# Narrow attentions: head operands written to DRAM by head, read back 48 partitions at a time; bias first; output products of batch 0 ahead of the last evacuation

## The reference, cut to what matters

```
h   = norm(x)
q   = (h @ Wq + bq) * scale           # 2 x 256 rows, 16 heads of 16
k,v = src @ Wk + bk, src @ Wv + bv    # 2 x 512 (L2, L3) or 2 x 768 (L0) rows
p   = softmax(q @ k.T + mask)         # per batch and head
x   = x + gate * ((p @ v) @ Wo + bo)
```

## Time and profile before

| | us |
|---|---|
| runs, median of 3 | 1135.85 (1135.51 to 1137.48) |
| profiled execution, its own time | 1132.89 |
| span of that execution in the trace | 1131.1 |
| L0a: first instruction, first score, last output product | 14.8, 52.1, 176.3 |
| L2a: first instruction, first score, last output product | 848.3, 878.3, 965.4 |
| L3a: first instruction, first score, last output product | 967.4, 1003.9, 1091.4 |

### The profile page before, as it was taken

One profiled execution on the slowest core, in us unless ns is written; L12 is line 12 of the kernel. 1 busy time (PEld: TensorE's weight loads), 2 busy tenths in 40 slices (PEclk: granted clock), 3 DMA queues, 4 the chain that ended last, 5 costly groups with the idle time before them and its releaser, 6 DMA issues. The chain is left out here.

```text
span 1131.1 us, 17854 instructions
## 1 busy us (share of the span) xinstructions
PE 956.8 (85%) x6548; PEld 809.0 (72%) x6548; DVE 817.2 (72%) x1624; ACT 603.5 (53%) x1367; POOL 336.1 (30%) x325
## 2 busy tenths in 40 slices
PE   4888886569999999997899999998586898478958
PEld 3666665558888889887778989987475566465647
DVE  3377767976787878787578787877664787757865
ACT  2488873034555555553355555655424786257842
POOL 4255541441112222221111222200005454534520
PEclk8889997888999999998899999999788799688989
DMA  5984106140001111111000111000305930296120
GB/s 180 252 130 63 12 1 247 56 162 1 15 24 38 38 39 38 38 38 39 1 4 36 38 38 38 2 1 1 117 1 123 169 44 1 59 191 73 13 80 19
DMA packets 37810, 69.49 MB, mean 61 GB/s; under 512 B 7414, under 2 KB 23288, under 8 KB 35036
## 3 DMA queue, kind: packets, MB, share of 16 engines
q1 hardware_dynamic: 37724, 68.35, 24.7%
HBM read 57.31 MB, written 11.02 MB: 60 GB/s over the span
## 5 line engine op out<-in xcount | busy, mean ns | idle before, releaser
L1230 ACT CAST L1a_probsT_hi<-L1a_bank 128x512 fp32r<-128x512 f32 x128 | 68.8, 589 | 94.3 <-PE L1a_bank L1111 94.3
L1069 POOL TENSOR_SCALAR L1a_wo_hi<-L1a_stage 128x512 fp32r<-128x512 f32 x16 | 10.3, 646 | 363.2 <-PE L1a_sums L74 355.6
L1347 DVE TENSOR_REDUCE L1a_top<-L1a_scores 128x2 f32<-128x1024 f32 x64 | 78.2, 1222 | 36.1 <-PE L1a_scores L74 36.1
L1262 ACT ACTIVATE L1a_probs<-L1a_scores,L1a_neg_max 128x512 f32<-128x512 f32 x128 | 86.8, 684 | 30.6 <-DVE L1a_bias_shifted L1351 25.6
L1285 DVE TENSOR_TENSOR L1a_probsT_lo<-L1a_bank,L1a_probsT_hi 128x512 fp32r<-128x512 f32 x128 | 82.0, 682 | 0.1
L72 PE MATMUL L1a_bank<-L1a_probsT_hi,L1a_v_hi 128*128 128x256 f32 x256 | 73.2, 286 | 9.2 <-DVE L1a_probsT_lo L1285 9.2
L1232 ACT ACTIVATE L1a_attended_hi<-L1a_bank,L1a_cols 128x256 fp32r<-128x256 f32 x64 | 30.5, 476 | 90.4 <-PE L1a_bank L74 90.4
L72 PE MATMUL L1a_bank<-L1a_w_hi,ctxT_hi 128*128 128x256 f32 x256 | 76.5, 299 | 1.1 <-DVE latT_lo L1303 1.0
L74 PE MATMUL L1a_bank<-L1a_w_hi,ctxT_lo 128*128 128x256 f32 x256 | 73.7, 288 | 0.0
L73 PE MATMUL L1a_bank<-L1a_w_lo,ctxT_hi 128*128 128x256 f32 x256 | 73.6, 288 | 0.0
L390 POOL TENSOR_SCALAR L0a_probs<-L0a_probs,L0a_inverse 128x768 f32<-128x768 f32 x64 | 57.2, 906 | 52.9 <-DVE L0a_inverse L641 52.9
(11 more groups left out here) (409 smaller groups left out, 3160.8 us busy)
## 6 DMA issues: line engine op xcount, KB each, us to landing
L1a_stage<-in_L_w SPq DMA_DIRECT2D x15, 1024.0 KB, 4.8
L0m_fold_wq<-in_L_wq SPq DMA_DIRECT2D x2, 2048.0 KB, 19.8
L0a_k_stack<-L0a_k_dram SPq DMA_DIRECT2D x12, 192.0 KB
L0a_w_qkv<-L0a_k_dram SPq DMA_DIRECT2D x12, 192.0 KB
L0a_probs<-in_L_wo SPq DMA_DIRECT2D x1, 2048.0 KB, 9.7
L0a_probsT<-in_L_wo SPq DMA_DIRECT2D x1, 2048.0 KB, 11.2
L0m_stage<-in_L_wm SPq DMA_DIRECT2D x4, 512.0 KB, 5.8
L0m_fold_bias_k<-in_L_bias_k SPq DMA_DIRECT2D x2, 1024.0 KB, 15.4
```

The lines of the kernel that those rows point to most:

```text
L1230: nc.scalar.copy(out, source).then_inc(ring.hi_done, 1)
L1262: nc.scalar.activation(probs[:, g % 2, qt, :], scores[:, qt, :], ACT.Exp, bias=neg_max[:, g % 2, qt:qt + 1], accum_out=row_sum[:, g % 2, q ...
L1347: link(nc.vector.tensor_reduce(top[:, :], scores[:, :, :], AX.X, ALU.max))
```

## The change

1. The DRAM copies have a new layout: `q_dram` and `k_dram` are [octet, head, 48, n], each head with its three groups of 16 rows in the order of the stack. So the high keys and the high queries are written twice: 6 writes an octet in place of 4, each from 128 partitions into 8 blocks of 16 rows; keys first, then the mask, then the queries (each with its own wait).
2. An octet comes back in 4 transfers of 48 partitions x 4 heads and 2 mask rows: 6 in place of 14. The mask rows are issued first, ahead of the wait for the writes. `q_stack` is [128, 2, 4, 256], even and odd heads apart.
3. Loading and splitting: bias and mask are loaded and made right behind the first weight piece; the output weight is split after the keys and queries are evacuated; gate and output bias are loaded and waited for later.
4. POOL clears only the 16 of 32 columns of `v` that stay zero.
5. The output tiles of batch 0 wait only for the products of batch 0, tile 2 only at its last quarter for the last one; DVE adds the output bias to x ahead of the last evacuation.

```diff
-        q_dram = nc.dram_tensor(f"{name}_q_dram", [2, D, ROWS], F32).ap()
-        k_dram = nc.dram_tensor(f"{name}_k_dram", [2, D, B * nk], F32).ap()
+        q_dram = nc.dram_tensor(f"{name}_q_dram", [OCTETS, 8, 3 * DN, Q], F32).ap()
+        k_dram = nc.dram_tensor(f"{name}_k_dram", [OCTETS, 8, 3 * DN, nk], F32).ap()
+        Q_PARTS, K_PARTS = (0, 1, 0), (0, 0, 1)
...
             def write(o):
                 b, kt = divmod(o, KT)
-                ring.wait_evacuated(sp, max(front.index(("q", kt)), front.index(key_jobs[kt, b][-1])))
-                rows = slice(kt * P, (kt + 1) * P)
-                for part in range(2):
-                    for of, at, n, to in ((qT[part][:, kt, :], b * Q, Q, q_dram), (kT[part][:, kt, :], b * nk, nk, k_dram)):
-                        sp.dma_start(to[part, rows, at:at + n], raw(of[:, at:at + n])).then_inc(written[o], 16)
+                ring.wait_evacuated(sp, front.index(key_jobs[kt, b][-1]))
+                for c, part in enumerate(K_PARTS):
+                    heads = k_dram[o, :, DN * c:DN * c + DN, :]
+                    sp.dma_start(heads, raw(kT[part][:, kt, b * nk:(b + 1) * nk])).then_inc(written[o], 16)
                 if o == 0:
                     sp.wait_ge(mask_ready, 1)
-                    sp.dma_start(mask_dram, raw(mask_row[:, :, :])).then_inc(written[o], 16)
+                    sp.dma_start(mask_dram, raw(mask_row[:, :, :])).then_inc(mask_written, 16)
+                ring.wait_evacuated(sp, front.index(("q", kt)))
+                for c, part in enumerate(Q_PARTS):
+                    heads = q_dram[o, :, DN * c:DN * c + DN, :]
+                    sp.dma_start(heads, raw(qT[part][:, kt, b * Q:(b + 1) * Q])).then_inc(written[o], 16)
...
                 for a in range(2):
-                    for c, (kp, qp) in enumerate(((0, 0), (0, 1), (1, 0))):
-                        row = 64 * a + 16 * c
-                        for to, of, at, n in ((k_stack[r][row:row + 16, :, :], k_dram[kp], b * nk, nk),
-                                              (q_stack[r][row:row + 16, a:8:2, :], q_dram[qp], b * Q, Q)):
-                            heads = of[kt * P:(kt + 1) * P, at:at + n].rearrange("(t a r) n -> a r t n", a=2, r=DN)[a]
-                            sp.dma_start(raw(to), heads).then_inc(stack_loaded[r], 16)
                     row = 64 * a + 48
                     sp.dma_start(raw(k_stack[r][row:row + 1, :, :]),
                                  mask_dram[0:1, b:b + 1, :].broadcast_to([1, 4, nk])).then_inc(stack_loaded[r], 16)
+                sp.wait_ge(written[o], 96)
+                for a in range(2):
+                    rows = slice(64 * a, 64 * a + 48)
+                    sp.dma_start(raw(k_stack[r][rows, :, :]), k_dram[o, a:8:2, :, :].rearrange("t r n -> r t n")).then_inc(stack_loaded[r], 16)
+                    sp.dma_start(raw(q_stack[r][rows, a, :, :]), q_dram[o, a:8:2, :, :].rearrange("t r n -> r t n")).then_inc(stack_loaded[r], 16)
...
-                    nc.gpsimd.memset(v[:, :, :], 0.0).then_inc(padding_set, 1)
+                    padding = v[:, :, :].rearrange("p t (h d) -> p t h d", d=32)[:, :, :, DN:32]
+                    nc.gpsimd.memset(padding, 0.0).then_inc(padding_set, 1)
...
-            ring.wait_evacuated(pe, job_of["V", units - 1, 0])
             for t in range(RT):
-                job = o0 + t
+                job, own = o0 + t, quads * (t // 2 + 1) - 1
+                if t == 0:
+                    ring.wait_evacuated(pe, job_of["V", own, 0])
+                if t == 2:
+                    ring.wait_evacuated(pe, job_of["V", own - 1, 0])
                 for quad in range(quads):
+                    if t == 2 and quad == quads - 1:
+                        ring.wait_evacuated(pe, job_of["V", own, 0])
```

More of the change, by code:

```diff
@@ L227, in narrow_attention @@
                    w_qkv[:, :, :, :].rearrange("p s i n -> p (s i n)")[:, 0:4 * nk].rearrange("p (t n) -> p t n", t=4)]
-        q_stack = [ph.sb(f"q_stack{i}", [P, 8, Q], F32R) for i in range(2)]
+        q_stack = [ph.sb(f"q_stack{i}", [P, 2, 4, Q], F32R) for i in range(2)]
         score_slots, probs_slots, small_slots = (4, 8, 8) if nk == S else (2, 6, 8)
@@ L349, in _ @@
                         write(other)
-                sp.wait_ge(written[o], 64 if o else 80)
                 sp.wait_ge(cleared[r], 3)
+                if o == 0:
+                    sp.wait_ge(mask_written, 16)
                 if o >= 2:
@@ L508, in _ @@
                 parts.scale(nc, act, ring)
-            for n, i in enumerate(WEIGHTS):
+            for n, i in enumerate(WEIGHTS[:3]):
                 if parts and not parts.plain and n == 2:
@@ L513, in _ @@
                 nc.scalar.mul(w[0][i], stage[:, i, :], 1.0 if i else cfg["scale"]).then_inc(w_hi, 1)
-            act.wait_ge(small_loaded, 64)
-            if cfg["gated"]:
-                nc.scalar.activation(gate[:, :], gate[:, :], ACT.Tanh).then_inc(gate_ready, 1)
             act.wait_ge(bias_ready, 1)
@@ L524, in _ @@
                                      bias=bias[:, column:column + 1]).then_inc(ring.hi_done, 1)
+            for i in WEIGHTS[3:]:
+                act.wait_ge(loaded[i], 16)
+                nc.scalar.copy(w[0][i], stage[:, i, :]).then_inc(w_hi, 1)
+            act.wait_ge(small_loaded, 32)
+            if cfg["gated"]:
+                nc.scalar.activation(gate[:, :], gate[:, :], ACT.Tanh).then_inc(gate_ready, 1)
             act.wait_ge(padding_set, 2)
@@ L551, in high_v @@
                 if unit == 0:
-                    act.wait_ge(written[0], 80)
+                    act.wait_ge(mask_written, 16)
                 job = job_of["V", unit, 0]
@@ L604, in _ @@
                 low(job, job, out, column, n)
+            for n, i in enumerate(WEIGHTS[3:], 3):
+                dve.wait_ge(w_hi, n + 1)
+                nc.vector.tensor_tensor(w[1][i], stage[:, i, :], raw(w[0][i]), ALU.subtract).then_inc(w_lo, 1)
             if cfg["bias_values"]:
@@ L616, in low_v @@
                     for o in range(OCTETS):
-                        dve.wait_ge(written[o], 64 if o else 80)
+                        dve.wait_ge(written[o], 96)
                 b, quad = divmod(unit, quads)
```

30 lines of the change are left out of this document (18 added, 12 removed).

## The result

The changed kernel takes 1161.5 us (median of 4 runs, 1159.7 to 1162.9), the kernel before, run beside it, 1135.7: a ratio of 1.0227, with an interval of 1.0205 to 1.0249. The change costs 25.9 us. The forecast was 1180, +44.5: the sign and the place were right, the size was not. The profiled execution of after has a span of 1159.5 us, 28.4 longer than the one of before.

The account below looks back on a forecast made before the run. PE, busy 85% of the span, was taken as the bound, with gains only where it idles, chiefly waiting for DMA-paced stacks. L2a +13.6, L3a +14.7, L0a +19.5, ends -3.3 gave +44.5: 1177.4, median 1180 us, range 1131 to 1212.

Parts of the forecast that it names:

- Eight engines: Stack writes to DRAM: leading counts 8 and 128, the smaller taken, so eight DMA engines a write, at most 200 GB/s.
- W = 131: Rate of a new stack write to DRAM: 131 GB/s taken, with 65 and 200 kept as ends; forecast's chance 0.49.
- rival B: Stack writes: eight engines, each at its full 25 GB/s; +3.0 us, 1139 us; chance 0.18.
- Rival C: Stack writes: eight engines in step, 16 partitions apart, crowd a few paths, 109 GB/s; +69, 1205 us; chance 0.15.
- The loads, 180: Octet loads of 48 partitions: 180 GB/s, so 6.6 us (L0a 8.7) for 9.5 (12.0).
- rival E: Octet loads of 48 partitions no faster than 131 GB/s; +14 us on any case; no chance of its own.
- the fixed part: Octet 0, first write issue to first load issue: 1.7 us beyond the bytes' own time, taken from the kernel before.
- Bias first: Front of narrow phases: L2a keys out at 858.0, queries 860.3, against 862.65; L0a's PE gets 4.6 us back.
- The wait before octet 1: PE waits behind queued writes: 16.5 us in L2a, 16.9 in L3a, 13.7 in L0a; +14.1, +13.8, +13.7.
- L0a: First narrow phase: first score +5.8 us behind queued weights, octet 1 wait +13.7; together +19.5.
- The ends: End of three narrow phases: output tiles right behind the last product, 1.10 us each; -3.3 us.
- The sum: Whole kernel: L2a +13.6, L3a +14.7, L0a +19.5, ends -3.3: +44.5 us.

Follow-up runs that it names:

- experiment 9: Changed kernel with the three parts side by side in DRAM, octets loaded by 128-partition transfers instead of 48 (scores not the reference's): 1103.5 us, 0.9738 of before.
- experiment 6: Changed kernel with the three parts side by side in DRAM, L1a's four DVE output-bias additions moved behind the value evacuations: 1124.1 us, 0.9885 of before.
- experiment 4: Changed kernel with the writes of octets 2 and 3 issued behind octet 1's loads instead of ahead: 1158.6 us, 1.0214 of before.

## Why the prediction was right in sign and wrong in size

- **Eight engines: right,** counted exactly as foreseen, 8 packets under 512 B a write and half of the share. By the Trainium skill ("DMA: Bandwidth & Descriptors", why a DMA increments its semaphore by 16) a transfer uses the largest number of engines up to 16 that divides the slowest dimension of both sides; the counts 57, 97 and the earlier trace rows agree.
- **The rate of a new write, W = 131: wrong,** measured 181 to 200, rival B. The failed step is "Eight engines with blocks of 16 rows each work on eight partitions at a time, which is nearer to the 16 of that row than to the 128 of the write's. I take W = 131". That row is one of loads, and its slowness is one of loads to few partitions (experiment 9); for writes read from 128 partitions an engine's pace comes to 25 GB/s. Rival C's 109 is wrong too: it was an estimate from the ports of the Trainium skill ("SBUF — State Buffer", section on the DMA port swizzle) for eight engines 16 partitions apart, while the page itself (section "Can I just issue two DMAs to hit both halves?") goes by the partitions that a single transfer spans, here all 128; the trace has 181 to 200.
- **The loads, 180: too fast,** 147, between the forecast and rival E. Octet 0 came out right by errors that cancel: in L2a the first load was issued 9.35 us after the first write (forecast 10.7), the loads lasted 9.9 (9.05), and the first score, taken from the start of the output products of the layer ahead, moved by -0.6 (44.9 us before, 833.4 to 878.3; 44.3 after, 844.9 to 889.2) against -0.5 forecast. At 181 to 200 GB/s the 1.18 MB take 5.9 to 6.5 of the 9.35, so the fixed part was about 3 us (an estimate) and not the 1.7 that was carried over from before. In L3a +0.7 against +0.9.
- **Bias first: right in the front.** Set back by the 11.5 us that L2a starts later (859.75 against 848.27 of SP's first issue), keys went out at 858.4 and queries at 861.1, forecast 858.0 and 860.3. The warning that the operation may wait for POOL at its new place came true in L2a: 1.53 us.
- **The wait before octet 1: right in kind, too long,** 11.6 in L2a and L3a for 16.5 and 16.9. Rival B with W = 200 would have had 7.2 and 7.6 (+4.8 and +4.45). The 4 us between have a name that the forecast had left out: "Octets 2 and 3 come at the quick load rate with no writes ahead: no wait" is true of their waits, but octet 2's loads ran beside octet 1's. Held back, 8.28 and 8.25 are left, within 1.1 of rival B. The path there was another than forecast. The forecast had writes for 27.0 us from the first score and 3.3 us of loads behind them; in L2a the writes were issued from 8 us before the first score, the loads of octet 1 11.3 us after it, and these took 14.0.
- **L0a: mostly wrong.** First score +4.2 for +5.8; before octet 1 a wait of 2.4 for 13.7. Octet 1 was there 30.1 us after the first score and not 40.4; PE wanted it after 27.7. W is most of the miss in the wait, since the forecast's own sum has 1.3 with W = 200; but for the first score that sum has +1.7, and the other 2.5 us came from the loads (12.8 us from first issue to score for 11.15) and from a first load 0.8 later.
- **The ends: right in sum,** -0.9, -1.3 and -0.6 us for -1.1 each: no idle time of PE is left between last product and output tiles (177.12 us in L0a). No wait of PE in the trace names the split output weight or the halved clearing; no run alters these alone.
- **Left out: what happens beside the change.** L1a's 3.4 us also come and go in one unchanged kernel (experiment 6); the 1.7 us up to L1a and the 1.1 at the end were not traced to a cause. The medians lie 25.9 apart, the profiled executions 28.4.
- **The sum.** First scores and octet 1 together: L0a 7.5 for 19.5, L2a 8.2 for 13.6, L3a 9.2 for 14.7; ends -2.7 for -3.3. That is +22.2 for +44.5, and 6.2 beside it. With W = 200 and all else as forecast the sum was rival B's +3.0. So of the 28.4 us, 25 came from what the forecast had too small or at nothing: fixed part, loads and queue order of octet 0 (8.2), octet 1 (10.4), the ends (0.6) and the stretches beside the change (6.2). A W that was too slow stood in for them; that the time fell inside the range is in good part luck.

## What to carry to other kernels

Before a DRAM layout is chosen for few and large loads, look at what it does to the writes: whether their slowest dimension on both sides still is a multiple of sixteen. Here one swap of two dimensions in DRAM gave both the full writes and the few loads. It is worth 37 to 39 us and turned a change that lost 2.3% into one that wins 1%. Where a buffer's writes must also be out before the buffer is reused, another order may only move the wait, as in experiment 4; and a rate measured for loads to few partitions says nothing of writes from many.

## What the runs showed of the hardware

- The rate of loads went with the partitions they cover, at full share of the engines: 16 partitions 124 to 131 GB/s, 48 partitions 147, 128 partitions 333 to 430. Writes from 128 partitions came to 25 GB/s an engine, on eight (197 to 200) as on sixteen (396), in long stretches. Octet 0's own writes on eight got 133 to 181 in three places and 208 in after's L0a (36 to 40 us).
- Transfers that one queue was given 2 us apart share the engines: PE's wait for octet 1 was 3.3 and 3.4 us shorter in two phases when octet 2's loads were held.
- Some of DVE's operations from SBUF to SBUF stand still while POOL clears or subtracts: 128x2 elements took 0.16 to 0.33 us in L0a with the bias first, 1.53 or 5.03 in L2a, 1.25 in L3a, and four additions 2.95 or 6.62 in one kernel. The low parts of weights (L598, 0.64 us each) were not held beside the same clearings. The Trainium skill ("SBUF — State Buffer", section "Who interferes with whom") says that DVE and GpSimd share a pair of ports, held for a whole instruction, that `tensor_scalar` can take it, and that a DVE instruction with two inputs in SBUF contends only with a GpSimd instruction that reads SBUF. The trace agrees in all three: the bias operation ended with a clearing, the additions were long beside a subtraction, and L598 ran through clearings, which only write. It shows besides that DVE may miss its turn between three clearings in a row. The long and the short value differ by 3 to 4 us in a stretch, as much as most of the edits tried here were worth.
